# Attention scores for the row maxima computed in four 64 x 64 tiles of TensorE, over half of the keys at a time, with the maxima transposed once per two slots

## The reference

```python
q = _qdq(x) @ _qdq(wq).T + bq                  # x: layer-normed, 8 x 56 x 256
kv = cond @ wkv.T + bkv                        # cond: 8 x 1500 x 256
k, v = jnp.split(kv, 2, axis=-1)               # 16 heads of 16
attn = jax.nn.softmax(jnp.einsum('bnhd,bmhd->bhnm', q, k) * scale, axis=-1)
o = jnp.einsum('bhnm,bmhd->bnhd', attn, v).reshape(B, N, C)
out = _qdq(o) @ _qdq(wp).T + bp
...
x = x + jnp.tanh(g_xattn[0]) * out
x = x + jnp.tanh(g_ffn[0]) * ffn(_layernorm(x))   # top 2 of 16 experts, capacity 128, and a shared one
```

## Time and profile before

| | us |
|---|---|
| median of three runs | 405.36 (404.94 to 405.92) |
| profiled execution | 400.01 |
| its span | 398.2 |
| TensorE busy | 356.4 |
| VectorE busy | 301.3 |
| ScalarE busy | 251.9 |
| TensorE's granted clock, mean | 0.98 |

### The profile page before, as it was taken

How to read it: one execution, slowest core, us unless ns; L and a number is a source line. 1 busy time by engine, 2 the same in 40 slices (tenths; PEclk the granted TensorE clock), 3 DMA queues, 4 the chain that set the end, 5 groups by cost and what they waited for, 6 DMA issues and landing times.

```text
span 398.2 us, 14047 instructions
## 1 busy us (share of the span) xinstructions
PE 356.4 (90%) x5821; PEld 266.2 (67%) x5821; DVE 301.3 (76%) x654; ACT 251.9 (63%) x414; POOL 106.8 (27%) x100
## 2 busy tenths in 40 slices
PE   0896899999999998998999999898986877999994
PEld 0673468658767765865776686586663656888883
DVE  3889886775685676677377667666988698999994
ACT  3475477776677676777467776567762265677671
POOL 6141463132022232303023230001000022745541
PEclk9999699999999999999899999999999899999998
DMA  8869994474185277247317305555100005954101
GB/s 252 204 153 196 231 184 125 83 166 106 68 151 162 56 117 193 83 73 163 107 54 123 102 15 85 114 151 169 55 3 3 0 1 201 253 162 129 49 0 48
DMA packets 34561, 45.67 MB, mean 115 GB/s; under 512 B 4043, under 2 KB 30347, under 8 KB 34371
## 3 DMA queue, kind: packets, MB, share of 16 engines
q1 hardware_dynamic: 33443, 43.74, 45.7%
q0 software_dynamic: 640, 0.78, 1.0%
q10 hardware_dynamic: 416, 0.26, 0.3%
HBM read 25.08 MB, written 0.47 MB: 64 GB/s over the span
## 4 chain that ended last, share of the span: by engine, by line
PE 75%; DVE 12%; issue 5%; DMA 3%; ACT 2%; POOL 2%; DVEq 0%; ACTq 0%; POOLq 0%
PE PS L1046 37%; PE PS L1112 10%; PE PS L1089 9%; PE PS L1123 7%; PE PS L1389 3%; PE PS L1348 3%; DVE mx L808 2%; PE PS L1099 2%; PE PS L1372 1%; DMA arena<-place_far 1%; DMA x_in<-x 1%; DVE KN L757 1%; DVE st L711 1%; DVE mtop L812 1%; DVE cT L729 1%
## 5 line engine op out<-in xcount | busy, mean ns | idle before, releaser
L808 DVE TENSOR_REDUCE mx<-PS 112x1 f32<-112x500 f32 (+1 forms) x128 | 114.3, 934 | 55.6 <-PE PS L1089 55.4
L508 ACT ACTIVATE PT_all<-PS 128x1344 f32<-128x1344 f32 x64 | 82.5, 1289 | 10.4 <-PE PS L1112 10.3
L1046 PE MATMUL PS<-cT,wkvT 128*128 128x500 f16 x288 | 71.8, 386 | 17.9 <-POOL zero L404 11.2
L1046 PE MATMUL PS<-wkvT,cT 128*125 128x256 f16 x576 | 74.3, 281 | 0.0
L1046 PEld LDWEIGHTS PS<-wkvT,cT 128*125 128x125 f16 x576 | 66.2, 140 | 5.3 <-issue 0.5
L1046 PEld LDWEIGHTS PS<-cT,wkvT 128*128 128x128 f16 x288 | 27.5, 99 | 50.8 <-POOL zero L404 11.1
L397 POOL TENSOR_TENSOR cT<-c_in,cT 128x1000 f16<-128x1000 f32 x18 | 37.5, 2084 | 88.9 <-ACT cT L486 88.9
L493 ACT ACTIVATE KN<-PS,col_in 128x500 f16<-128x500 f32 x48 | 32.5, 677 | 41.4 <-PE PS L1046 41.4
L1089 PE MATMUL PS<-arena,QC 96*112 96x500 f16 x192 | 52.4, 380 | 3.5 <-issue 3.3
L1112 PE MATMUL PS<-QC,arena 98*128 98x112 f16 x768 | 49.2, 214 | 3.0 <-ACT QC L528 2.9
L500 ACT ACTIVATE V<-PS 125x512 f32<-125x512 f32 x48 | 28.7, 598 | 32.1 <-PE PS L1046 32.1
(11 more groups left out here) (211 smaller groups left out, 435.3 us busy)
## 6 DMA issues: line engine op xcount, KB each, us to landing
arena<-KN SPq DMA_DIRECT2D x144, 125.0 KB, 3.7
c_in<-ctx SPq DMA_DIRECT2D x24, 500.0 KB, 4.6
cT<-W SPq DMA_DIRECT2D x11, 352.0 KB
c_in<-W SPq DMA_DIRECT2D x6, 352.0 KB
cT<-W SPq DMA_DIRECT2D x11, 176.0 KB
arena<-place_far SPq DMA_DIRECT2D x1, 1568.0 KB, 8.5
c_in<-W SPq DMA_DIRECT2D x6, 176.0 KB
PT_all<-L_xattn_wkv SPq DMA_DIRECT2D x1, 512.0 KB, 6.0
```

Of the source, the lines that this page charges most:

```text
L508: act.activation(PT_all[:, u % 4, :].rearrange("p (c k) -> p c k", c=CH), PS[:, 3:6, 0:4 * TP], ACT.Exp, scale=SCORE).then_inc(s["exp_done ...
L808: dve.tensor_reduce(mx[:, u % 2, k:k + 1], PS[0:TP, k:1 + k * (CH - 1), 0:CW], AX.XY, ALU.max).then_inc(s["red_done"], 1)
L1046: ins = mm(out_, w(a, h), x_(b, h), start=first and k == 0, stop=last and k == len(todo) - 1)
```

## The change

Two consecutive slots (2q, 2q+1) now handle the same two pairs of heads, the first over one half of the keys (750) and the second over the other. The scores of a slot are four tiles of 64 rows by 64 columns: two row groups (`a`, one for each head of a pair: rows 0 to 47 and 64 to 113 of the stacked operands) by two column groups (`c`, one for each pair). Each tile has 750 columns in three pieces (238 or 256), so a slot has twelve matmuls. The pieces are ordered so that the two row groups never write the same bank in neighbouring pieces (`STEADY`); the last seven slots have another order (`LAST`). The stack of keys and of queries has 114 rows with a gap for this, and six DMAs per tile in place of three.

VectorE reduces twice 750 columns, both after all scores of the slot; the maxima are made after the odd slot, for two pairs at once. They are turned with two matmuls in the next even slot and copied by ScalarE in one operation. Turned scores and exp come one slot later than before, outputs move from odd to even slots, and the fills are dealt to the slots anew. One more slot follows at the end. A value tile is projected with 128 columns of context (of which 125 count) in all but two tiles of batch 0, and so waits in two cases for the lo half of the next chunk. Context buffers have 1504 columns, and some constants are made in another way. The result is stored with three DMAs, the last of them on ScalarE's queue, in place of four on SP's.

```diff
+QR = 96
+KR = 114
+HB = 64
+HEADS = (slice(0, 48), slice(HB, KR))
+KEYS_AT = ((0, 0, DH, 0), (0, HB, DH, DH), (1, DH, DH, 0), (1, HB + DH, DH, DH), (0, PW, PW, 0), (0, QR + 2, DH, DH))
+PIECES = (((0, 0, 256), (256, 256, 256), (512, 512, 238)), ((786, 0, 238), (1024, 238, 256), (1280, 494, 256)))
+STEADY = ((0, 2), (1, 1), (0, 0), (1, 2), (0, 1), (1, 0))
+LAST = ((0, 0), (0, 1), (0, 2), (1, 1), (1, 2), (1, 0))
...
 def slot_fills(u):
-    order = ("K0", "K1"), ("K2",), ("K3", "V0"), ("K4",), ("K5", "V1"), ("V2",), ("V3", "V4"), ("V5",)
+    order = ("K0",), ("K1", "K2"), ("K3",), ("V0", "K4"), ("K5",), ("V1", "V2"), ("V3",), ("V4", "V5")
     fills = [(name[0], b + 1, int(name[1])) for name in order[i]] if b + 1 < B else []
-    if i % 2 == 1 and 3 <= u <= SLOTS - NPAIR:
-        fills = (fills or [None]) + [("P", 0, (u - 3) // 2)]
+    if i % 2 == 0 and 4 <= u <= SLOTS - NPAIR:
+        fills = (fills or [None]) + [("P", 0, (u - 4) // 2)]
...
             def stack_keys(n, oh, c):
-                for k in (0, 2, 1):
-                    if k == 1:
+                for a in range(2):
+                    if a == 1:
                         need(sp, "kl_done", n * 6 + oh * CH + c + 1)
-                    sp.dma_start(KS[PW * k:PW * k + PW, n % 2, 4 * oh:4 * oh + 4, c * CW:(c + 1) * CW],
-                                 KN[:, oh, c, k % 2, :]).then_inc(stacked[oh][c], 16)
+                    for half, row, rows, first in KEYS_AT:
+                        if half == a:
+                            sp.dma_start(KS[row:row + rows, n % 2, 4 * oh:4 * oh + 4, c * CW:(c + 1) * CW],
+                                         KN[4 * first:4 * (first + rows), oh, c, a, :]).then_inc(stacked[oh][c], 16)
...
             def act_slot(u):
-                if 2 <= u:
-                    exp(u - 2)
+                if 3 <= u:
+                    exp(u - 3)
                 if fills and fills[0]:
                     evacuate(fills[0])
-                if 1 <= u <= SLOTS:
-                    augment(u - 1)
+                if 2 <= u <= SLOTS and u % 2 == 0:
+                    augment(u // 2 - 1)
                 if i % 2 == 1 and i < 6 and b + 2 < B:
                     context_hi(b + 2, i // 2)
                 if len(fills) > 1:
                     evacuate(fills[1])
...
+            def reduce(u, a):
+                q, h = divmod(u, 2)
+                col = PIECES[a][0][0]
+                need(dve, "sc_ready", 2 * u + 2)
+                need(dve, "nm_done", q - 1)
+                dve.tensor_reduce(mx[:, q % 2, h, a:a + 1], S_flat[:, col:col + HALF], AX.X, ALU.max).then_inc(s["red_done"], 1)
...
             def dve_slot(u):
                 if u < SLOTS:
                     reduce(u, 0)
                     reduce(u, 1)
-                    maxima(u)
+                    if u % 2 == 1:
+                        maxima(u // 2)
                 keys_lo_of(fills, 0)
                 keys_lo_of(fills, 1)
...
             def scores(u):
+                i, h = i - u % 2, u % 2
...
+                early = u > SLOTS - NPAIR
+                if early:
+                    need(pe, "red_done", 2 * u - 1)
+                else:
+                    need(pe, "red_done", 2 * u)
+                for k, (a, piece) in enumerate(LAST if early else STEADY):
+                    if early and k == 2:
+                        need(pe, "red_done", 2 * u)
+                    col, key, n = PIECES[a][piece]
+                    key += h * HALF
+                    if (a, piece) == (1, 0):
+                        pe.wait_ge(s["sc_ready"] if early else s["mid_done"], 2 * u + 1 if early else u + 1)
+                    for c in range(2):
+                        at = (i + c) * TP + a * S
+                        last = mm(PS[HB * c:HB * c + HB, col // 512, col % 512:col % 512 + n], QC[HEADS[a], b % 2, at:at + HB],
+                                  KS[HEADS[a], b % 2, i + c, key:key + n], start=True, stop=True, tile_position=(HB * a, HB * c))
...
+            def turn_maxima(q):
+                need(pe, "nm_done", q + 1)
+                if maxima_bank(q) == 0:
+                    need(pe, "red_done", 2 * (2 * q + 2) + 1)
...
+                for a in range(2):
+                    last = mm(PS[QR:QR + 2, maxima_bank(q), a * 128:a * 128 + SROWS], nm16[:, q % 2, :, a], ident16[0:SROWS, 0:SROWS],
+                              start=True, stop=True, tile_position=(0, QR))
...
             def pe_slot(u):
                 if u < SLOTS:
                     scores(u)
-                if early and u <= SLOTS:
-                    turn_maxima(u - 1)
+                turns = 2 <= u <= SLOTS and u % 2 == 0
+                if early and turns:
+                    turn_maxima(u // 2 - 1)
...
                 if fills and fills[0]:
                     project(fills[0])
-                if 1 <= u and not early:
-                    turn_maxima(u - 1)
+                if turns and not early:
+                    turn_maxima(u // 2 - 1)
                 if len(fills) > 1:
                     project(fills[1])
...
-                if 1 <= u <= SLOTS:
-                    turned_scores(u - 1)
+                if 2 <= u <= SLOTS + 1:
+                    turned_scores(u - 2)
```

More of the change, by code:

```diff
@@ L70, in bank_uses @@
     bank = {(name[0], 0, int(name[1])): b for name, b in zip(FIRST, (4, 5, 6, 0, 4, 5, 6, 0, 4, 5, 6, 4))}
-    for u in range(SLOTS + 2):
+    for u in range(SLOTS + 3):
         for k, use in enumerate(slot_fills(u)):
@@ L411, in _ @@
             for oh in range(NH):
-                for k in (0, 1, 2):
-                    gp.wait_ge(s["qn_ready"], 1 + k // 2)
-                    gp.dma_start(q16[PW * k:PW * k + PW, 4 * oh:4 * oh + 4, 0:TP], qn[:, oh, k // 2, 0:TP]).then_inc(s[f"q_stacked{oh}"], 16)
+                for half, row, n_rows, first in QUERIES_AT:
+                    gp.wait_ge(s["qn_ready"], 1 + half)
+                    gp.dma_start(q16[row:row + n_rows, 4 * oh:4 * oh + 4, 0:TP],
+                                 qn[4 * first:4 * (first + n_rows), oh, half, 0:TP]).then_inc(s[f"q_stacked{oh}"], 16)
             def queries(n, k):
@@ L1071, in project_values @@
                 bank = take(("V", n, v))
-                need_lo(pe, n, v // 2)
+                over = n > 0 and v % 2 == 1 and v < 5
+                need_lo(pe, n, v // 2 + over)
                 for k in range(2):
                     t = 2 * v + k
-                    last = split3(PS[0:KP, bank, k * D:(k + 1) * D], lambda a, h: cT[:, n % 2, a, h, t * KP:(t + 1) * KP],
+                    w = KP if n == 0 and t in (3, 7) else 128
+                    last = split3(PS[0:w, bank, k * D:(k + 1) * D], lambda a, h: cT[:, n % 2, a, h, t * KP:t * KP + w],
                                   lambda a, h: wkvT[:, a, h, D:2 * D])
@@ L1080, in scores @@
                 b, i = divmod(u, NPAIR)
-                need(pe, "aug_done", min(u - 1, SLOTS - NPAIR))
-                if i % 4 == 0:
-                    need(pe, "qc_done", 2 * b + i // 4 + 1)
-                for c in range(CH):
-                    if i % 4 == 0:
-                        pe.wait_ge(stacked[i // 4][c], 48 * (b + 1))
-                    if c < 2:
-                        need(pe, "red_done", 2 * (u - 1) + c + 1)
-                    mm(PS[0:TP, c, 0:CW], QC[0:QR, b % 2, i * TP:(i + 1) * TP], KS[0:QR, b % 2, i, c * CW:(c + 1) * CW],
-                       start=True, stop=True).then_inc(s["sc_ready"], 1)
@@ L1092, in turn_maxima @@
-            def turn_maxima(u):
-                need(pe, "nm_done", u + 1)
-                if maxima_bank(u) == 0:
-                    need(pe, "red_done", 2 * (u + 1) + 1)
+                i, h = i - u % 2, u % 2
+                need(pe, "aug_done", min((u - 1) // 2, (SLOTS - NPAIR) // 2))
+                if i % 4 == 0 and h == 0:
+                    need(pe, "qc_done", 2 * b + i // 4 + 1)
+                if i == 2 and h == 0:
+                    need(pe, "qc_done", 2 * b + 2)
+                if i % 4 == 0:
+                    for c in (range(2) if h == 0 else range(2, CH)):
+                        pe.wait_ge(stacked[i // 4][c], 16 * len(KEYS_AT) * (b + 1))
@@ new lines, in scores @@
+                early = u > SLOTS - NPAIR
[14 more added lines that the diff above has]
+                                  KS[HEADS[a], b % 2, i + c, key:key + n], start=True, stop=True, tile_position=(HB * a, HB * c))
+                    if (a, piece) == (0, 2 if early else 1):
+                        last.then_inc(s["sc_ready"], 1)
+                    elif (a, piece) == (0, 2):
+                        last.then_inc(s["mid_done"], 1)
@@ L1108, in turned_scores @@
                     need(pe, "kl_done", 6)
[L1109 removed]
+                need(pe, "aug_done", u // 2 + 1)
                 need(pe, "exp_done", u)
                 for t in range(KT):
[L1112 to L1113 removed]
+                    last = mm(PS[:, 3 + t // 4, (t % 4) * TP:(t % 4 + 1) * TP], KS[0:KR, b % 2, i, t * KP:t * KP + 128],
```

(3 more changed lines are left out.)

129 lines of the change are left out of this document (63 added, 66 removed).

## The result

| | before | after |
|---|---|---|
| median, us | 405.15 (4 runs, 401.24 to 405.92) | 412.85 (4 runs, 407.23 to 421.24) |
| profiled execution, its span | 400.01, 398.2 | 407.23, 405.5 |
| TensorE, VectorE, ScalarE busy | 356.4, 301.3, 251.9 | 354.5, 286.1, 242.8 |

The account below looks back on a forecast made before the run. TensorE bounds the middle, VectorE the last slots. Batches 1 to 5 -5.2, batch 6 -1.9, batch 0 -0.9, start +1.5, last slots and tail +2.0, store -0.1: -4.6 on 400.0 profiled, 400.8 as median; range 390 to 409.5 us.

Parts of the forecast that it names:

- What bounds the kernel: TensorE's own work sets the middle, busy 32.3 of a batch's 33.00 us; VectorE sets the last eight slots.
- The scores, s: Score time per slot in four tiles: 0.42 us against 0.64 before, bounds 0.31 and 0.72.
- The turn's wait: Slots 2 and 4, batches 1 to 5: the turn waits 0.70 and 0.62 us, giving back 1.3 of 2.4 a batch.
- Maxima, values with 128 columns: Middle batches: four turns of 0.14 us per batch go; value projections with 128 columns for 125 change by 0.
- The middle in sum: Batches 1 to 6 together: predicted -7.1 us, from -5.2 for batches 1 to 5 and -1.9 for batch 6.
- The start: First slots: more key copies and a later context load, against no turns in slots 0 and 1; +1.5 us, -1.5 to +4.
- The last slots: Last eight slots: 2.45 us a slot against 2.42, and outputs move into slot 56; together +0.7 us.
- The tail: After the last maxima: two exps one after the other ahead of the outputs; +1.3 us, to 2.1.
- the second one: Rival: row tiles don't overlap or weight loads set the pace, s 0.64 to 0.72; +5 to +9, 410 to 414 us; chance 0.18.
- The third: Rival: scores shrink, but the start's late context load costs +4 and more copies delay instruction loads; 403 to 406 us; chance 0.15.

Follow-up runs that it names:

- the kernel without the wait: Changed kernel, a slot's last score piece (1, 0) written over (1, 1) in bank 2 without its `mid_done` wait, from slot 1, last seven slots excepted; 409.51 us, single execution.
- the kernel that turns the order round: Kernel with both repairs, plus ScalarE's slot 56 evacuation behind the weight copies and GpSimd's weight low half waiting for the last maxima but one; 401.95 us, ratio 0.9976.
- the kernel with both repairs: Changed kernel with context 2 loads moved between SP's key copies and GpSimd's additions held until the second maxima; 401.25 us, ratio 0.9933 to before.
- the loads earlier: Changed kernel with only the context 2 loads moved between SP's key copies at the start; 404.76 us, ratio 1.0023 to before.
- the one with two column tiles doubled: Changed kernel with scores in two column tiles over all 114 rows, no row groups, each matmul of slots 0 to 56 issued twice; scores segment 1.40 us.

## Why the prediction was wrong

**What bounds the kernel**: right. TensorE back to back in the middle, VectorE in the last slots.

**The scores, s**: the first step that failed. I took 0.42; it is 0.67 in all. Full overlap of the four tiles was right, and that loads don't matter, for which the earlier trace rows had stood. Around it 0.25 us were missed (the split is an estimate from the kernel without the wait: rounds from 103.50, 103.63 and 103.74, the next segment at 103.95): 0.12 is the wait on `mid_done` in the diff, an instruction of the change to which I gave no price at all; the three rounds take 0.35, not 0.31; and the way in and out costs 0.10 each, where I gave 0.10 for both together. The way in could be had from the trace of before, as the 0.09 by which turned scores are longer ahead of outputs.

**The turn's wait**: right in place and cause, too large in size. I had 0.70 and 0.62 at s = 0.42, which is 0.45 and 0.37 at 0.67; the slots 2 and 4 are 0.23 and 0.15 longer than those of batch 6 (4.31 and 4.23 against 4.08). The sum of eight steps was 0.22 too long. That the wait takes back what scores gain there was shown by the kernel without `mid_done`, where it grows from 0.17 to 0.30.

**Maxima, values with 128 columns**: right. Turns ahead of outputs cost 0.01 to 0.13 for two, and 24 matmuls of values take 2.63 us (109.54 to 112.17) for 2.61 before (23.70 to 26.31).

**The middle in sum**: -6.8 for -7.1 by chance. Clean batches gave 6 x 0.23 = 1.4, fewer stalls 5.4, of which 3.5 hang on one slot of the one trace of before.

**The start**: the second step that failed, +8.7 for +0.6. The load went out at 41.02 (I had about 40) and was there 4.4 us later (I had 5), and the chain ScalarE, K2, turn was the one that I named. But I had netted it to +1.5 with a bound of +4, by setting waits for keys against it; the wait was 6.08 us, and 4.5 us of half clock followed (before has a stretch of half clock as well). And I saw no second wait: in the earlier trace rows the small operations take 0.16, and I had not looked for the longest of their line in batch 0. It was there before, 2.20 us beside GpSimd's addition:

```profile
47.84 2.34 POOL L438 TENSOR_TENSOR x<-x_in,row_in 112x1024 f32<-112x1024 f32 x1
...
48.01 2.20 DVE L817 SCALAR_TENSOR_TENSOR nm<-mtop,nm 112x1 f16<-112x1 f32 x1
```

**The last slots**: the third, +4.7 for +0.7. The pace was 2.54 (I had 2.45). The outputs in slot 56 (1.3 us) were taken to fit beside VectorE's reduction for the most part, and did not; ScalarE's queue behind them was not followed, and cost 0.5 more, as the kernel that turns the order round shows. The clash and the half clock (1.7) were not foreseen.

**The tail**: +0.6 for +1.2, as predicted in kind. The second exp is there (302.73 and 304.96), and the outputs wait for it 1.38; the kernel with both repairs has 8.1 us from the last maxima to the last outputs' copy, for 6.6 before. What hides part of it is that the first three quarters of the following step are done meanwhile.

**The rivals**: the second one had the sign, and 412.85 is in its 410 to 414, yet by another way: s reached its 0.64 to 0.72, but neither did the tiles fail to overlap nor did the loads pace them, and batches became shorter, not longer. The third had the place, at the start, and not the size; its other half, delayed instruction loads, is shown by no run: TensorE's "issue" stalls between 70 and 270 us are 3.3 to 6.8 us in the kernels with this middle, 4.5 before. I had weighed them as if one excluded the other, and ended the range at 409.5. That 0.2% could be told from no change was wrong too: the interval of the first set is 1.8% wide. Start and last slots, 13.4 us for my 1.3, are more than the 7.1 that I expected of the middle: even with the scores as forecast the kernel would have been slower.

## What to carry to other kernels

Give every wait in a diff a price, those within one engine too: a matmul's result is not there when the next starts, and a wait that looks satisfied since its matmul was issued first can cost a fifth of a short segment (0.12 of 0.57). Where an operation moves in one queue, follow all that stands behind it on each engine to the next thing that TensorE waits for, and look at the longest, not the mean, of each small operation on a critical chain: it tells who it shares something with. When a regression is a sum of two waits in a row, repair them together before judging either.

## What the runs showed of the hardware that I had not expected

- Four tiles of 64 x 64 overlap almost in full: row groups start 0.01 us apart, and a slot of 750 columns a tile takes 0.45 us with nothing in its way, 0.76 with column tiles alone. The Trainium skill (TensorE: Matmul & The Clock Gate, Part 3: Packing small matmuls — row/col tiling) says that tiles start about 4 ns apart and run together; the trace, which gives times to 0.01 us, agrees, and I had not weighed it.
- A VectorE operation of 0.16 us with two inputs from SBUF lasted 5.55, 6.05 and 4.44 us (in after, with the loads earlier, with both) while GpSimd ran operations back to back, and got its turn only after others of them had ended in between (in after the ends at 56.1 and 57.8 pass it by); in the kernels where GpSimd waits it takes 0.16. The Trainium skill (SBUF — State Buffer, SBUF: two separate sides) has the lock that VectorE and GpSimd share for an instruction's whole length; the trace agrees with that, and shows besides that the one who waits is not always served at the next end of the other's operations: in after three of them end before it is, and then it is served between two `cT` operations, at 59.9. The reductions, whose one input is in PSUM, kept their 0.93 us: two of them take 1.78 from 54.37 on in the kernel with both, beside GpSimd's operations from 53.56.
- Kernels that differ only in the scores had 1.9 to 16.5 us of TensorE stalls between 70 and 270 us that the profile names "issue" (0.4 in the one with two column tiles doubled). In kernels with the same middle they come back in the same slots. What sets them stays open.
